# VectorE's order in a fused Mamba-2 and product-key expert block: the scan's read-out, sum and gate ahead of row groups 20 and 21 instead of behind them

## The reference

```
x = layernorm(u + mamba2(u))       # in-projection, 4-tap convolution, chunked scan, gate, RMS norm, out-projection
x = layernorm(x + experts(x))      # MLP to 256 features h, product keys, 8 heads x top 8 of 4096 experts

# mamba2: y = scan(x*dt, A*dt, B, C) + x*D ; y = y*silu(z) ; y = rmsnorm(y)*scale ; y @ W_out
# experts, for a token with private features h:
z   = h . down_embed[indices]      # 64 picked rows a token, 256 numbers each
z   = silu(z * softmax(scores))    # one coefficient a row
out = sum z * up_embed[indices]    # the same rows, 512 numbers each
```

## Time and profile before

| | |
|---|---|
| median of 3 runs | 3157.48 us (3154.82 to 3172.02) |
| profiled execution, its own time | 3151.04 us |
| its span, first to last instruction | 3149.2 us |
| busy share: TensorE, VectorE, ScalarE, GpSimd | 89%, 88%, 65%, 65% |
| mean granted TensorE clock | 0.953 of full speed |

### The profile page before, as it was taken

The page is one execution under the profiler, slowest core; times in us unless marked ns, Lnnn a source line. Parts: engine busy times, 40 slices in busy tenths (PEclk is TensorE's granted clock), DMA queues, the critical chain, the costliest instruction groups (busy, mean ns, idle before and its releaser), DMA issues.

```text
span 3149.2 us, 44785 instructions
## 1 busy us (share of the span) xinstructions
PE 2790.8 (89%) x11776; PEld 1737.3 (55%) x11776; DVE 2777.5 (88%) x10160; ACT 2049.7 (65%) x6513; POOL 2062.7 (65%) x2056
## 2 busy tenths in 40 slices
PE   7989899998898999999899989899898999898863
PEld 4565456655555655555566545556555565555541
DVE  3489899998899999999899989999999999899986
ACT  3466766666776666676666676666676666677642
POOL 0066666676676667666667666666766666766676
PEclk9999999999999999999999999999999999999986
DMA  8088888888888888888888888888888888888888
GB/s 284 23 263 275 270 279 273 277 290 282 272 285 265 270 292 287 276 282 277 265 277 297 273 276 271 273 278 290 284 277 268 276 272 288 283 278 281 277 303 272
DMA packets 189855, 856.76 MB, mean 272 GB/s; under 512 B 36192, under 2 KB 39392, under 8 KB 189088
## 3 DMA queue, kind: packets, MB, share of 16 engines
q0 software_dynamic: 163840, 805.44, 77.0%
q1 hardware_dynamic: 19104, 34.87, 3.2%
q10 hardware_dynamic: 6656, 13.60, 1.2%
HBM read 845.38 MB, written 8.39 MB: 271 GB/s over the span
## 4 chain that ended last, share of the span: by engine, by line
PE 38%; DVE 32%; DMA 9%; POOL 9%; issue 7%; ACT 5%; POOLq 0%; SPq 0%; DVEq 0%; ACTq 0%
DVE bank L1143 14%; POOL ring L276 9%; DMA ring<-embed,idx 9%; PE bank L500 8%; DVE ring L1129 8%; PE bank L359 7%; DVE xc L974 6%; PE bank L339 5%; PE bank L441 4%; PE bank L488 4%; PE bank L368 3%; ACT xc L679 1%; PE bank L376 1%; PE bank L307 1%; ACT xskip L691 1%
## 5 line engine op out<-in xcount | busy, mean ns | idle before, releaser
L276 POOL DMA_INDIRECT ring<-embed,idx x2048 | 2061.4, 1007 | 1074.8 <-issue 532.3
L1143 DVE SCALAR_TENSOR_TENSOR bank<-ring,coef,bank 128x512 f32<-128x512 f32 x1312 | 992.4, 756 | 7.4 <-issue 0.2
L1129 DVE SCALAR_TENSOR_TENSOR ring<-ring,hcur 128x256 f32<-128x256 f32 x2048 | 823.8, 423 | 138.5 <-DMA ring<-embed,idx 136.1
L645 ACT ACTIVATE coef<-prob,zp 128x1 f32<-128x1 f32 x2048 | 456.0, 286 | 630.8 <-DVE ring L1129 625.4
L500 PE MATMUL bank<-ring,diag_c 128*128 128x512 f32 x1344 | 672.8, 631 | 115.9 <-ACT diag_c L654 101.3
L463 PE MATMUL bank<-zs,w_up 128*128 128x128 f32 x4096 | 502.2, 287 | 69.2 <-ACT zs L767 65.8
L463 PEld LDWEIGHTS bank<-zs,w_up 128*128 128x128 f32 x4096 | 496.2, 203 | 110.2 <-ACT zs L767 91.8
L500 PEld LDWEIGHTS bank<-ring,diag_c 128*128 128x128 f32 x1344 | 247.2, 199 | 379.2 <-issue 223.7
L974 DVE SCALAR_TENSOR_TENSOR xc<-raw,taps,xc 128x128 f32<-128x128 f32 x960 | 266.2, 351 | 102.6 <-ACT xc L679 102.5
L339 PE MATMUL bank<-w_in,ut 128*128 128x512 f32 (+1 forms) x768 | 285.8, 524 | 4.0 <-ACT seg L667 3.9
L654 ACT ACTIVATE diag_c<-cst,coef 128x128 f32<-128x128 f32 x672 | 234.8, 394 | 48.4 <-PE bank L500 38.0
(11 more groups left out here) (144 smaller groups left out, 3422.2 us busy)
## 6 DMA issues: line engine op xcount, KB each, us to landing
ring<-embed,idx POOLq DMA_INDIRECT x2048, 4.6
ring<-uT SPq DMA_DIRECT2D x4, 2048.0 KB, 14.2
ut<-uT SPq DMA_DIRECT2D x32, 256.0 KB, 6.5
zs<-u SPq DMA_DIRECT2D x32, 256.0 KB, 5.6
out<-acc SPq DMA_DIRECT2D x32, 256.0 KB, 4.6
w_up<-W_upT ACTq DMA_DIRECT2D x1, 4096.0 KB, 13.0
w_in<-W_in ACTq DMA_DIRECT2D x1, 2560.0 KB, 17.4
w_in<-W_in ACTq DMA_DIRECT2D x1, 2048.0 KB, 22.0
```

Source lines behind the costliest of these rows:

```text
L276: pool.indirect_dma_start(out=ring[:, k % RING, :], out_offset=None, in_=embed, in_offset=bass.IndirectOffsetOnAxis(ap=idx[:, half, k:k + ...
L645: m = act.activation(coef[:, k:k + 1], prob_v[:, k:k + 1], ACT.Silu, scale=zp[:, k:k + 1])
L1129: m = dve.scalar_tensor_tensor(out=ring[:, k % RING, 0:DP], in0=ring[:, k % RING, 0:DP], scalar=1.0, in1=hcur[:, :], op0=ALU.mult, op1=ALU ...
L1143: dve.scalar_tensor_tensor(out=total if n == len(DVE_ROWS) - 1 else running[:, :], in0=ring[:, k % RING, DP:ROW], scalar=coef[:, k:k + 1], ...
```

## The change

In VectorE's `tile`, `old(20, 21)` moves behind the six instructions of the scan's end. No instruction is added or dropped, and no other engine's program changes.

```diff
@@ -1236,7 +1236,7 @@
                 if ahead:
                     scaled_x(i + 1)
                     masked_products(i + 1)
-                old(18, 19, 20, 21)
+                old(18, 19)
                 if ahead:
                     scan_out(i + 1, 0)
                     scan_out(i + 1, 1)
@@ -1244,6 +1244,7 @@
                     scan_add(i + 1, 1)
                     scan_gate(i + 1, 0)
                     scan_gate(i + 1, 1)
+                old(20, 21)
                 softmax(i, first)
                 if not first:
                     weigh_all(i - 1, NGRP - 1, False)
```

## The result

| | before | after |
|---|---|---|
| median | 3156.15 us (3148.27 to 3172.02, 4 runs) | **3341.63 us** (3337.61 to 3344.03, 4 runs) |
| ratio | | **1.058**, 95% interval 1.0548 to 1.0612 |
| span of the profiled execution | 3149.2 us | 3338.8 us |
| mean granted TensorE clock | 0.953 | 0.932 |

The changed kernel is 5.8% slower. The forecast was 3340 us.

The account below looks back on a forecast made before the run. The prediction took a slack-free loop through TensorE, ScalarE and VectorE as the bound. L441's 5.2 us delay plus 0.9 us of clock, times 30 calls, gave 183 us over 3151.0, plus 6.4 for the median: 3340 us, range 3272 to 3385.

Parts of the forecast that it names:

- The wait at L1000: VectorE ahead of the scan's end: idle 3.81 us every call until `xdec_ok`, about 114 us in all.
- Groups 20 and 21: VectorE behind the scan: their DMA waits vanish, 4.38 us of work remain, and dot 63 is done 6.06 us later.
- ScalarE's chain: ScalarE from dot 63 to `turn_y`: 5.24 us, all work, nothing in it can start sooner.
- L441: TensorE's out-projection: starts at 1769.0 instead of 1763.81, 5.2 us later.
- The clock: TensorE's L441: a 3.4 us low-clock stretch falls wholly into it, about 0.9 us a call, ends 0 and 2.5.
- the page's bound: TensorE's warm-up under 1% of span: 11 us more in all instead of 27, a time some 16 us lower.
- The gathers: GpSimd's queue: row 1's gather 5.4 us later, dot 6 and `back_sum` at most that; `new(1)` covered by 0.8 us.
- The rival that the gathers bind: New tile's rows land 2 us later still, TensorE's `new(1)` waits for `back_sum`: 7.5 us a call, 3382 us; 12%.
- The shorter way to y: ScalarE copies the transposes at once and L441 follows y, 1.9 us sooner: 57 us faster, 3100 us; 5%.
- VectorE's waits cancel: VectorE is the bound; its stretch ends 2.5 us later but L974's 3.5 us wait swallows it: 3157 us; 5%.
- The absorbed case: TensorE's 1.3 us wait for h at L481 vanishes, clock costs nothing: 3.9 us a call, 3274 us; 8%.
- The sum: Whole call: 5.2 + 0.9 = 6.1 us in 30 calls, 183 us, giving 3340 us, 5.8% slower.

Follow-up runs that it names:

- run 1: Changed kernel with ScalarE's second half of `end_decay` moved ahead of the coefficients of groups 18 and 19: 3691.17 us against 3642.64 for the kernel before, 1.0143.
- Run 10: Changed kernel with ScalarE's `turn_y` moved ahead of the two halves of `state_decay`: 3265.72 us against 3154.44 for the kernel before, 1.0367.
- Run 9: Changed kernel with only group 21 behind the scan, group 20 staying ahead: 3284.63 us against 3154.44 for the kernel before, 1.0427.
- run 8: Changed kernel, four weighings ahead of the scan, ScalarE's `turn_y` and TensorE's first half of the out-projection ahead of what waits for dot 63: 3174.84 us, 1.0067 of before.
- run 12: Run 8's kernel with `back_sum`'s addition moved from behind dot 7 to right behind dot 5: 3182.83 us against 3158.50 for the kernel before, 1.008.
- run 4: Changed kernel plus five unread 512-column matmuls a call on TensorE ahead of L441: 3658.67 us against 3642.64 for the kernel before, 1.0047.

## Why the prediction was right

**The wait at L1000.** Predicted 3.81 us idle and 0.04 for the release in 30 calls, 114 us in all; measured 3.90 in the call shown and 118.3 us in all (31 waits). What the prediction did not see is that `xdec_ok` has a rival at L1000: with `end_decay` out of the way (run 1) VectorE still waited 118 us there. So the size was right, but on that chip it is much the same without `end_decay`.

**Groups 20 and 21.** Dot 63 was to be 6.06 us later. It is 6.10 us later on average (11.94 against 5.84), with no wait for a row at dots 60 to 63. The three parts of it (wait, scan in front, row waits that vanish) are each seen in the rows. The waits for rows did not go from the run, though: L1129 waits 134.7 us for them against 136.1. The 1.3 us a call at dots 60 and 63 are gone, and dots 4, 15 and 16 of the new tile wait 1.9 us a call instead of 0.3.

**ScalarE's chain.** Predicted 5.24 us from dot 63 to `turn_y`, as in the one call; measured 5.17 on average. Run 10 shows that this chain is what L441 waits for: 3.9 us of it moved behind `turn_y` bring the call down by 2.5 us, until row 61's matmul takes over.

**L441.** Predicted 5.2 us later; 5.23 in the call shown (1768.66 - 1750.93 against 1763.81 - 1751.31), 5.37 on average.

**The clock.** Mis-sized. I took a low stretch of 3.4 us, as long as in the earlier trace rows, falling wholly into L441, and got 8.7 us for L441 and 0.9 us a call (8.7 - 7.7 is 1.0, which would have made some 3343 us; and a low stretch twice as long, 6.8 us, would have cost 2.8 us by the same working and not the 1.8 of the upper end). The low stretch lasted about 10 us, of which 3 to 4 lie in L441: 289.2 / 32 = 9.04 us, and L441 to L339 1.17 us longer. That the number came out near was luck of a kind: the stretch was three times as long, but most of it lay where TensorE had nothing to do. Run 9 shows the term's form: it is not in proportion to the delay, but is nearly all there at half of it.

The Trainium skill, page "TensorE: Matmul & The Clock Gate", Part 1, puts the warm-up below 1% of a typical kernel's span. Here L441 alone takes 289.2 us where 32 x 7.03 = 225 would do at full speed, 64 us or 1.9% of the span; so the measurement goes past that figure, and the 16 us by which the page's bound would have lowered my forecast would have made it worse (3324 against 3341.63 measured).

**The gathers.** Row 1's gather went out at 1759.81, 8.9 us after dot 59, where the prediction had 8.7 (1760.0 - 1751.31) and the kernel before 3.3: 5.6 us late, worked out as 5.4. Behind that I was wrong, in the harmless direction: I let dot 6 and `back_sum` move by up to the same 5.4 us and gave `new(1)` 0.8 us of cover. Dot 6 is 2.6 us later against dot 59 (1770.82 - 1750.93 against 1768.61 - 1751.31), `back_sum` 3.3 us on average, and it ends 3.7 us ahead of `new(1)`. Row 6 lands within 4.7 us of its gather, where it took 7.3 us (4.5 against 6.9 on average over the 26 calls). The rival that the gathers bind (3382 us) had so no ground.

**The other rivals.** The shorter way to y (3100 us) would need `turn_y` closer behind the last dot than before; it came 5.17 us behind it on average, 5.18 before. "VectorE's waits cancel" (3157 us) did not happen either: the wait at L974 stayed. But this rival held more truth than its 5%: runs 8 and 12 show that VectorE's own chain is level with TensorE's in the kernel before. It is a bound for any gain, not a cushion for a loss. The absorbed case (3274 us) fell: L481's wait for h did not vanish but grew, from 42.1 to 70.5 us.

**The sum.** Predicted 5.2 + 0.9 = 6.1 us in each of 30 calls, 183 us; measured 5.4 + 1.2 - 0.1 = 6.4, 190 us of span, and 185 us between the medians.

**Where the kernel before stands.** I had written that there is no slack on the loop for a delay. The runs add that there is none to be gained either by one step: three branches (ScalarE's copy and the out-projection; `back_sum`; dots 11 to 13 and ScalarE's copies of the in-projection) come out level there within some 0.5 us (`back_sum` ends 19.6 us after dot 59 and L441 20.1; L339 waits at most 0.3 us for L667). Moving the scan ahead never ended below 1.00 in the forms tried here (1.0067 at best where the kernel before takes about 3156 us, 1.0047 with filler on the others), so no version of this study beats the kernel before.

**What stays open.** No run took the parts "new wait" and "clock" apart cleanly: run 1 left the wait in place, and run 4 gave TensorE a higher clock than the kernel before has, both on chips where the kernel before takes over 3600 us. For the result they are read from the profile and from runs 8 to 10. Why those chips are slower, and why the change costs 4.0% on them instead of 5.8%, is not known. Nor is why the rows land later behind L974 in run 9, nor why VectorE still waited as long in run 1.

## What to carry to other kernels

An instruction that is moved ahead takes its wait along: what used to cover the wait now stands behind it, and with it everything that other engines' in-order queues hold back for that work. So before moving a producer ahead, look in the consumer's queue for what stands ahead of the consumer; here y was 1.9 us sooner and of no use, since ScalarE could not copy it before it had dots 60 to 63. Ask for all conditions of a waiting instruction as well: the view names the last one, and with that one gone another may be met as late (run 1). And where several branches come out level, each edit that shortens only one of them gains nothing, while an edit that lengthens one costs in full.

## What the runs showed of the hardware that I had not expected

- **Loads that miss the gathers land in half the time.** SyncE now issues the loads of u at 1758.55, in the pause of the gathers (DMA share 0.20 from 1756 to 1760). Before, they went out at 1760.78 among the rows. The page's list of DMA issues (size, median us to landing) has, for the kernel before:

```profile
ut<-uT SPq DMA_DIRECT2D x32, 256.0 KB, 6.5
zs<-u SPq DMA_DIRECT2D x32, 256.0 KB, 5.6
```

  and after:

```profile
ut<-uT SPq DMA_DIRECT2D x32, 256.0 KB, 2.9
zs<-u SPq DMA_DIRECT2D x32, 256.0 KB, 2.6
```

  The other runs bear it out. In runs 8, 9 and 12 the loads go out as early (7.6 to 7.8 us after dot 59) but among gathers, and the median of `zs` is 5.6 to 5.7 us; in run 10 the gathers pause, and it is 2.6. The rows' own median hardly changed (4.6 and 4.5 us), but row 6, which was under way together with these loads before, lands in 4.7 us instead of 7.3. I take this for the reason why `back_sum` was not as late as I allowed for; it was not tried by itself. It gained no time, since the loads were not waited for.
- **The clock stayed low through a stretch of sparse work.** After 4.4 us of idleness TensorE ran one row's two matmuls (2.08 us at half speed), idled 2.5 us and began L441, still at 0.50; it was back at full clock only some 4 us into L441. In run 4, with filler in the gap, L441's matmuls took 599 ns on average, against 739 in the changed kernel on such a chip.
- **Two chips took 3614 to 3650 us for a kernel that takes 3156 us elsewhere**, with the same busy time on VectorE, a lower mean granted clock and more busy time on TensorE (0.879 and 3007 us for the changed kernel, against 0.932 and 2815), and long stops that no semaphore of the program explains. Ratios differ there as well (1.040 instead of 1.058), so a time from one chip is only compared with the kernel before on the same chip.
